# Local attention of a four-part network on one core: scores as contractions of 64 rows, with maxima for eight heads in one reduction

## The reference

```python
h = shift_token(x)                       # half of the channels come from the token before
q, k, v = split(h @ wqkv)                # 128 -> 3 * 512, eight heads of 64
q, k = l2norm(q) * qs, l2norm(k) * ksc
q, k = rotary_xpos(q, k)
sim = einsum('bhwid,bhwjd->bhwij', q_window * 8, k_window_and_the_one_before)
sim = where((i < j) | (i > j + 64) | (j == -1), -max, sim)
o = einsum('bhwij,bhwjd->bhwid', softmax(sim), v_window_and_the_one_before)
x = x + o @ wo                           # then shift_token, layer norm, gated feed-forward
```

## Time and profile before

| | |
|---|---|
| median of 3 runs | 2175.99 us (2174.62 to 2183.37) |
| profiled execution, its own time | 2176.2 us |
| its span | 2174.4 us |
| PE, DVE, ACT, POOL busy over the span | 82%, 75%, 58%, 44% |
| mean granted TensorE clock | 0.929 |
| attention of local layer 0, first scores to first feed-forward matmul | 1321.3 to 1649.0 us |
| attention of local layer 1, the same | 1733.8 to 2062.1 us |
| one block of it in the steady state | 20.31 us |

### The profile page before, as it was taken

The page is one execution under the profiler, slowest core; times in us unless marked ns, Lnnn a source line. Parts: engine busy times, 40 slices in busy tenths (PEclk is TensorE's granted clock), DMA queues, the critical chain, the costliest instruction groups (busy, mean ns, idle before and its releaser), DMA issues. The chain is left out here.

```text
span 2174.4 us, 36880 instructions
## 1 busy us (share of the span) xinstructions
PE 1781.2 (82%) x12448; PEld 976.1 (45%) x12448; DVE 1635.1 (75%) x3467; ACT 1271.2 (58%) x2737; POOL 957.9 (44%) x773
## 2 busy tenths in 40 slices
PE   5888898865889998859943757999998899999875
PEld 2333333332344444424423424655655556566543
DVE  5999999995577777622235767999986689999775
ACT  5777877740344444414434236888884388888721
POOL 5777887761012222223431245555550255555311
PEclk8999999996899999959976878999999999999997
DMA  5333333312111111114235140000001000000010
GB/s 150 110 111 119 122 108 116 93 49 81 39 37 36 41 36 44 31 41 133 65 105 165 52 137 15 16 21 16 11 16 23 13 16 21 16 16 11 15 42 23
DMA packets 107401, 125.47 MB, mean 58 GB/s; under 512 B 28804, under 2 KB 79151, under 8 KB 106224
## 3 DMA queue, kind: packets, MB, share of 16 engines
q1 hardware_dynamic: 103120, 115.07, 18.7%
q0 software_dynamic: 4096, 8.06, 1.1%
HBM read 71.60 MB, written 38.11 MB: 50 GB/s over the span
## 5 line engine op out<-in xcount | busy, mean ns | idle before, releaser
L394 POOL TENSOR_TENSOR m_bu<-m_dtu,m_brow 128x1024 f32<-128x1024 f32 x128 | 299.8, 2358 | 55.6 <-DVE m_hs L818 53.9
L818 DVE TENSOR_TENSOR_SCAN m_hs<-m_ps_da,m_bu 128x1024 f32<-128x1024 f32 x128 | 292.3, 2283 | 3.0 <-POOL m_bu L394 2.5
L1363 ACT ACTIVATE a_pt<-a_ps_s 128x1024 f32<-128x1024 f32 x128 | 131.1, 1024 | 226.7 <-PE a_ps_s L1141 226.7
L523 PE MATMUL m_ps_y_ps<-m_prod,m_ident 128*128 128x512 f32 x512 | 243.1, 597 | 0.0
L2913 ACT ACTIVATE l_pe<-l_ps_s,l_nbias,l_qs 128x128 f32<-128x128 f32 x512 | 227.9, 459 | 1.6
L1480 DVE TENSOR_REDUCE a_mpad<-a_ps_s 128x4 f32<-128x1024 f32 x128 | 156.9, 1226 | 92.3 <-PE a_ps_s L1133 91.1
L1133 PE MATMUL a_ps_s<-a_heads 32*128 32x256 f32 x1024 | 187.5, 446 | 43.6 <-DVE a_mpad L1480 28.5
L670 ACT ACTIVATE m_ps_da<-m_dt,m_a_neg 128x510 f32<-128x510 f32 x256 | 166.0, 681 | 74.3 <-DVE m_hs L818 73.4
L1141 PE MATMUL a_ps_s<-a_qm,a_heads 32*128 32x256 f32 x1024 | 184.7, 437 | 1.8 <-ACT a_pt L1363 1.4
L1067 POOL TENSOR_TENSOR a_rstd<-a_ve,a_mhalf 128x2 f32<-128x2 f32 x48 | 33.8, 705 | 303.0 <-DVE a_ve L1438 163.3
L828 DVE TENSOR_TENSOR m_prod<-m_hs,m_ps_c_ps 128x1024 f32<-128x1024 f32 x128 | 153.6, 1200 | 12.1 <-PE m_ps_c_ps L509 12.1
(11 more groups left out here) (339 smaller groups left out, 4252.1 us busy)
## 6 DMA issues: line engine op xcount, KB each, us to landing
m_brow<-state_rows SPq DMA_DIRECT2D x64, 512.0 KB, 4.3
slots<-m_void SPq DMA_DIRECT2D x16, 516.0 KB, 5.4
l_near<-l_v SPq DMA_DIRECT2D x64, 128.0 KB, 2.3
e_xs<-slots SPq DMA_DIRECT2D x16, 258.0 KB, 2.8
ys<-m_void SPq DMA_DIRECT2D x8, 512.0 KB, 5.3
qk<-a_qk SPq DMA_DIRECT2D x16, 256.0 KB, 2.0
a_heads<-qk SPq DMA_DIRECT2D x64, 64.0 KB
ew_w<-in_w SPq DMA_DIRECT2D x2, 2048.0 KB, 11.8
```

The source lines that it names most:

```text
L394: nc.gpsimd.tensor_tensor(bu[s % 4][:, :, :], dtu[p][:, :, :], b2, ALU.mult).then_inc(bu_rd, 1)
L523: last = pe.matmul(y_ps[:, h, :], ident[:, :], prod[d % 3][:, h, :], start=False, stop=(s == NS - 1))
L818: dve.tensor_tensor_scan(hs[s % 4][:, :, :].rearrange("p h t -> p (h t)"), da[s % 2][:, :, :, :].rearrange("p h q t -> p (h q t)"), bu[s % ...
L1363: nc.scalar.activation(pt[t % 2][:, :, :], s2[:, :, :], ACT.Exp).then_inc(exp_rd, 1)
```

## The change

The buffer `kT` loses its zero half: `k_copy` is one copy of 128 rows, and the two memsets at the start of the phase go. `scores` now handles a whole chunk, all eight heads. The two score banks become one tensor `s_ps` of two banks, the even heads in bank 0 and the odd heads in bank 1. Each head's product contracts over its own 64 rows only: rows 0 to 63 for an even head, 64 to 127 for an odd one. There are 8 such matmuls in chunk 0 and 16 in chunk 1, each of 128 columns, after two mask matmuls. `maxima` reduces both banks in one instruction for eight heads. The next chunk's scores therefore wait until all eight exponentials of this one are done.

The orders of PE, ACT and DVE in `attend` are rewritten for this:

```diff
-                for i in range(2):
-                    nc.gpsimd.memset(kT[i][:, :, :, :], 0.0).then_inc(cleared, 1)
...
+                def scores(n, b, c):
+
+                    l, p, i = at[n], b % 2, NCH * b + c
+                    pe.wait_ge(l.xT_sb[Q], i + 1)
+                    pe.wait_ge(l.xT_sb[K], i + 1)
+                    at_least(pe, l.ex_rd, NH * i)
+                    bank = [s_ps[:, r, :].rearrange("p (j t) -> p j t", j=NP) for r in range(2)]
+                    side = [slice(r * HD, (r + 1) * HD) for r in range(2)]
+                    for r in range(2):
+                        pe.matmul(bank[r], identb[:, :], mask[:, c, :, :], start=True, stop=False, skip_group_check=True)
+                    for j in range(NP):
                         if c == 0:
+                            for r in range(2):
+                                last = pe.matmul(bank[r][:, j, :], qT[p][side[r], j, 0:P], kT[p][side[r], j, 0:P],
+                                                 start=False, stop=True, skip_group_check=True)
                         else:
+                            for q in range(2):
+                                q0 = P + q * HD
+                                for r in range(2):
+                                    last = pe.matmul(bank[r][side[q], j, :], qT[p][side[r], j, q0:q0 + HD],
+                                                     kT[p][side[r], j, q0 - HD:q0 + HD], start=False, stop=True,
+                                                     skip_group_check=True)
...
-                    for h in range(2):
-                        rows_ = slice(h * HD, (h + 1) * HD)
-                        nc.scalar.copy(kT[b % 2][rows_, h, :, c * P:(c + 1) * P],
-                                       qk_ps[rows_, K, :].rearrange("p (j t) -> p j t", j=NP)).then_inc(l.xT_sb[K], 1)
+                    nc.scalar.copy(kT[b % 2][:, :, c * P:(c + 1) * P],
+                                   qk_ps[:, K, :].rearrange("p (j t) -> p j t", j=NP)).then_inc(l.xT_sb[K], 1)
...
 # ScalarE, attend
+                    for c in range(NCH):
+                        if not first:
+                            o_copy(n, b - 1, c)
+                        if c == 1:
+                            p_copy(n, b, 0)
+                        elif not first:
+                            p_copy(n, b - 1, 2)
+                        exps(n, b, 2 * c)
+                        if last < 2:
+                            v_copy(n, b + 1, c)
+                        if c == 1 and last < 1:
+                            shift(n, b + 2)
+                        if last < 2:
+                            square(n, b + 1, c, Q)
+                        if c == 0:
+                            k_copy(n, b, 1)
+                        elif last < 2:
+                            k_copy(n, b + 1, 0)
+                        exps(n, b, 2 * c + 1)
...
 # VectorE, maxima
-                    dve.tensor_reduce(top[:, :], s_ps[u % 2][:, :].rearrange("p (h k) -> p h k", h=HU), AX.X, ALU.max,
+                    dve.tensor_reduce(top[:, :].rearrange("p (j r) -> p r j", r=2),
+                                      s_ps[:, :, :].rearrange("p r (j t) -> p r j t", j=NP), AX.X, ALU.max,
                                       negate=True).then_inc(l.top_s, 1)
```

More of the change, by code:

```diff
@@ L2734, in attend @@
                     if not first:
[L2735 to L2738, removed]
+                        transpose_p(n, b - 1, 3)
                         if last < 2:
@@ L2930, in attend @@
                 def attend(n, b, first=False, last=0):
[L2931 to L2963, removed]
+                    for c in range(NCH):
+                        if not first:
+                            o_copy(n, b - 1, c)
[4 more added lines that the diff above has]
+                        exps(n, b, 2 * c)
+                        if last < 2:
+                            v_copy(n, b + 1, c)
+                        if c == 1 and last < 1:
+                            shift(n, b + 2)
+                        if last < 2:
+                            square(n, b + 1, c, Q)
[4 more added lines that the diff above has]
+                        exps(n, b, 2 * c + 1)
+                        if c == 1:
+                            p_copy(n, b, 1)
+                        elif not first:
+                            p_copy(n, b - 1, 3)
+                        if last < 2:
+                            q_copy(n, b + 1, c)
+                            square(n, b + 1, c, K)
@@ L3092, in attend @@
                 def attend(n, b, first=False, last=0):
[L3093 to L3128, removed]
+                    for c in range(NCH):
+                        if c == 1 and last < 2:
+                            square_sums(n, b + 1, 0, K)
+                        elif c == 0 and not first:
+                            square_sums(n, b, 1, K)
+                        maxima(n, b, c)
+                        if last < 2:
+                            rotary(n, b + 1, c, Q)
+                        if c == 0:
+                            scale_k(n, b, 1)
+                        elif last < 2:
+                            scale_k(n, b + 1, 0)
+                        else:
+                            norm_stats(n, 0)
+                        divide(n, b, 2 * c)
+                        if last < 2:
+                            square_sums(n, b + 1, c, Q)
+                            rotary(n, b + 1, c, K)
+                            rotary_sum(n, b + 1, c, K)
+                        if not first:
+                            residual(n, b - 1, c)
+                        divide(n, b, 2 * c + 1)
```

78 lines of the change are left out of this document (28 added, 50 removed).

## The result

The changed kernel takes 2202.7 us in the median (2201.5 to 2208.8), the kernel before 2175.7 (2174.6 to 2183.4). The ratio is 1.0122, 95% interval 1.0092 to 1.0152: slower by 1.2%, 27 us. The prediction had the direction and the range, but 2189, only 13 us more. The profiled execution has a span of 2199.6 us against 2174.4, 25.2 more.

A forecast was written before the change was run, and what follows sets the result against it. No engine had much room, so the chain closing each chunk's loop was taken as the bound. A layer gains 9.9 - 0.2 - 3.0 = 6.7 us, two layers 13, on 2176.2 us: 2189, range 2150 to 2220.

The forecast's parts named there:

- Scores on PE: Scores take 1.65 us in chunk 0 and 1.55 in chunk 1; PE has 1.64 us less work a block.
- the rival without overlap: Last rival: row groups do not run side by side in the scores of both chunks; 2215 or 2241 us; chance 0.12.
- Loop of chunk 0: Chain from scores through weigh, transposes, q's projection, scale_k and k_copy to the next scores: 10.01 us, before 10.02.
- the rest behind the projection of k: PE's projection of k and the rest of its list up to the next scores: 2.82 us, in both loops.
- Loop of chunk 1: Exponentials ahead of v_copy on ACT, then shift, square, k_copy, projection of k and the rest: 11.01 us, before 10.29.
- Block, ends: Blocks 0 to 13 take 0.71 us more each; in each layer block 14 0.2 less, last block and tail 3.0 less.
- PE's work: Rival: PE's work sets the pace, 1.64 us a block come off, -49 us, 2127; chance 0.12.
- Chunk 1 did not go like chunk 0: Rival: chunk 1 also takes about 10.0 us, exponentials ending before v's projection is through; 2162 us; chance 0.24.
- A lower granted clock in the longer gaps: In PE's longer gaps: none expected, as gaps of 0.6 us leave the clock at 1.00; no term given.

The follow-up runs named there:

- pulling the heads apart: Changed kernel with the score products reordered, first all even heads, then all odd ones; ratio 1.0272.
- the key's copy first: Changed kernel; in chunk 1 ACT's copy of k stands before shift and square of q, PE's turn of k before the transpose of the residual; ratio 0.9976.
- the version with blocks of 19.62: Against the key's copy first: in chunk 1 the square of q stands ahead of the copy of k; ratio 0.9885.
- the filler: Changed kernel plus one unread matmul of 512 columns, 0.87 us, ahead of the projection of k in chunk 1; ratio 1.0062.
- nearly every second with 1.86: Against the key's copy first: on DVE in chunk 1 the rotation of k stands ahead of the sum of q's squares; ratio 1.0235.
- every one with 2.11: Changed kernel in its order, but with the scores of the kernel before: 128-row contractions, zero half in kT, two copies of k; ratio 1.0728.
- the half filler: Changed kernel plus one unread matmul of 256 columns, 0.43 us, ahead of the projection of k in chunk 1; one run, 2209.1 us.
- that last order: Against the version with blocks of 19.62: on PE the transposes of the probabilities stand ahead of the projection of k in both chunks; ratio 0.983.

## Why the prediction was right in the loops and wrong in the time

*Scores on PE.* Right: 1.62 and 1.56 us for 1.65 and 1.55. That they run side by side is shown by pulling the heads apart, and the rival without overlap falls away. Chunk 0's products took 1.09 us (1554.89 to 1555.98), not the 1.7 of sixteen loads in a line. The loads of different rows overlap: 156 loads of 0.187 us each, 29.2 together, fill only 9.5 us. From the groups of weight loads of the changed kernel, 1400 to 1600 us (busy us, mean ns of one, idle before):

```profile
L2656 PEld LDWEIGHTS l_ps_s<-l_kT,l_qT 64*128 64x128 f32 x156 | 9.5, 187 | 4.2 <-issue 4.2
L2623 PEld LDWEIGHTS l_ps_a<-t_wqkv,l_hT 128*128 128x128 f32 x38 | 7.2, 190 | 9.1 <-issue 9.1
```

The Trainium skill ("TensorE: Matmul & The Clock Gate", LDWEIGHTS) gives the time of one load as its columns over 1.2 GHz, whatever its rows. That the rows do not count the trace bears out, with 0.187 us for 64 rows and 0.190 for 128, though both are longer than the 0.107 that this makes. That the loads stand in a line was the prediction's own addition in its last rival.

*Loop of chunk 0.* Right within 0.18 us: 9.83 for 10.01. Each link is within 0.1, the largest difference being the rest behind the projection of k, 2.73 for 2.82.

*Loop of chunk 1.* Right: 10.99 for 11.01. The start of the exponentials came 0.13 later than reckoned, the links behind it 0.15 sooner in sum. Moving the copy of k, with its turn on PE, took 0.73 us off a block, so the chain is shown to set the pace, not only to fit. One word of the prediction needs mending. It blames the exponentials that stand ahead of `v_copy`. They still stand there with the key's copy first, where `v_copy` starts 5.26 us after the first mask (5.24 in the changed kernel), and in the version with blocks of 19.62. It is the shift and the square between `v_copy` and `k_copy` that made the late `v_copy` expensive.

*Block, ends.* 0.51 a block instead of 0.71 (26 blocks, 5.2 us less than forecast), blocks 14 0.9 lower, last blocks as forecast but for one fall of the clock.

*The rivals.* PE's work did not set the pace, as PE was idle for 17 us of 100. Chunk 1 did not go like chunk 0, 10.99 us against 9.83.

*The step that failed* is the sentence "A lower granted clock in the longer gaps would add to either; I expect none, as gaps of 0.6 us leave it at 1.00 now". The rows of before showed what gaps of 0.57 us do, and the forecast itself had a gap of over a microsecond. I carried the row across to a case that it doesn't show, and gave the clock no term. The runs have in its place: 1.65 us for each fall, 9.0 us in blocks 1 to 13, 1.65 in one tail, and 4.0 in the two blocks 0, where 8.8 and 8.7 us run at half clock instead of 2.6 and 3.1 (with the filler, 4.6 and 4.9 us do, and 2.7 of these 4.0 us are gone). With the wait filled, the ratio falls from 1.0122 on one chip and 1.0105 on another to 1.0062 (1.0037 to 1.0086). The forecast's 13 us are 1.0060; that the two meet so closely is in part luck, as the steady blocks cost some 4 us less than forecast and the two blocks 1 have 4.5 us more than before even with the filler. What the table has besides, 2.0 us before the local layers and 2.8 in the feed-forward parts, lies in unchanged code. The feed-forward parts were seen to vary by 0.7 and 3.7 us between two traces of the kernel before alone.

What stays open: which waits at which moments let the clock fall. Among blocks 2 to 13, two of twelve fall with 1.51 us, nearly every second with 1.86, every one with 2.11, and eight with the heads apart at 1.51. No single number of the rows orders these. But the falls of the changed kernel are not scattered: in its two traces and in that of the half filler the two slow ones of these blocks stand five apart in every layer, 105.8 us from one slow chunk to the next (1480.63 to 1586.39, 1842.35 to 1948.11), while the blocks between have the same wait at full clock. So it also counts when a wait comes. With what it has to coincide, no run here shows.

## What to carry to other kernels

When a change lengthens a wait of the matrix engine beyond any that the trace of before holds, price the clock as a term of its own: here each fall cost 1.65 us, and by the filler's ratio about half of the loss came from it. A chain that moves has as many queues behind it as there are engines. Write down the list of each, the small norms on GpSimd too. And when work is made cheaper, put what is left into the waits, since the order decides: the same scores gave 1.012 in one order and 0.983 in another. How the old scores would do in that last order was not run.

## What the runs showed of the hardware

Products of 64 rows and 64 columns run in quartets: 16 products of 128 columns, 32 passes, let the next instruction start 1.03 us after the first of them. With the row halves not alternating they need 1.53. The 8 products of 64 rows and 128 columns take 1.09 alternating and 1.64 otherwise.

The clock fell for 3.4 us (in places twice that) shortly behind a wait, and came back to 1.00 by itself while the loop went on. In the steady state of the changed kernel the two falls of a layer were 105.8 us apart, at waits like all the others. A filler of 0.87 us kept it up in the steady state, one of 0.43 did not.

A division of 512 elements on DVE takes 0.69 us alone and up to 1.57 beside GpSimd's sum of two tensors, a scaling 0.68 or 1.75.
